# Casting DMAs from DRAM to DRAM in place of a packing pass through SBUF, in an attention and FFN block on one core

## What is computed

```
x = x + proj(quantise(concat(self_attention, cross_attention)))   # 8 groups, 2 heads each, 128 wide
x = x + down(silu(gate(layernorm(x))) * up(layernorm(x)))         # hidden size 1408
```

```
W = (wq.astype(float32) - ZERO_POINT) * scale[:, None]     # ZERO_POINT = 128
```

## Time and profile before

| what | value |
|---|---|
| median of 3 runs | 1793.88 us (1792.93 to 1796.43) |
| the profiled execution's own time | 1795.76 us |
| its span in the trace | 1793.9 us |
| TensorE's mean granted clock | 0.977 of full speed |
| busy share of the span: PE, DVE, ACT, POOL | 93%, 76%, 78%, 63% |
| DMA queue of SP | 254.71 MB, 71.0% of 16 engines |

### The profile page before, as it was taken

How to read it: one execution, slowest core, us unless ns; L and a number is a source line. 1 busy time by engine, 2 the same in 40 slices (tenths; PEclk the granted TensorE clock), 3 DMA queues, 4 the chain that set the end, 5 groups by cost and what they waited for, 6 DMA issues and landing times.

```text
span 1793.9 us, 44172 instructions
## 1 busy us (share of the span) xinstructions
PE 1675.9 (93%) x15776; PEld 1230.4 (69%) x15776; DVE 1364.5 (76%) x3181; ACT 1399.3 (78%) x2944; POOL 1138.4 (63%) x1043
## 2 busy tenths in 40 slices
PE   1449999999999999999999999999999979999999
PEld 1437778878887887788788877787888534444444
DVE  8969888997998799889979987997777652323232
ACT  6888999999999999999999999999999622121211
POOL 1137788778788877887787788778877613030202
PEclk9669999999999999999999999999999989999999
DMA  5557799888888988888798878888999970112100
GB/s 183 177 190 125 147 159 166 147 148 161 153 157 144 172 152 148 160 161 148 148 166 152 151 151 176 146 148 172 176 196 205 196 229 0 67 74 98 42 24 24
DMA packets 671666, 257.41 MB, mean 143 GB/s; under 512 B 616288, under 2 KB 634976, under 8 KB 671456
## 3 DMA queue, kind: packets, MB, share of 16 engines
q1 hardware_dynamic: 671456, 254.71, 71.0%
HBM read 74.10 MB, written 29.51 MB: 58 GB/s over the span
## 4 chain that ended last, share of the span: by engine, by line
ACT 28%; PE 21%; DVE 19%; POOL 15%; issue 10%; SPq 4%; DMA 3%; ACTq 0%; DVEq 0%; POOLq 0%
POOL local L1129 10%; ACT local L1041 7%; ACT local L1038 7%; ACT local L961 5%; PE ps_s L727 5%; DVE w_raw L1199 4%; ACT local L948 3%; DVE local L1371 2%; POOL w_raw L1113 2%; SPq L614 2%; DVE sq_sum L1284 2%; PE ps_pj L844 2%; PE ps_pj L845 2%; PE ps_o L844 2%; PE ps_o L845 2%
## 5 line engine op out<-in xcount | busy, mean ns | idle before, releaser
L1129 POOL TENSOR_TENSOR local<-local 128x512 bf16<-128x512 f32 x512 | 594.0, 1160 | 258.6 <-ACT local L1041 258.2
L720 PE MATMUL ps_pj<-wide 128*128 128x256 bf16 (+1 forms) x5544 | 584.9, 255 | 6.7 <-DVE wide L1208 4.0
L720 PEld LDWEIGHTS ps_pj<-wide 128*128 128x128 bf16 x5544 | 468.8, 98 | 116.8 <-ACT local L961 7.5
L1038 ACT ACTIVATE local<-ps_s,neg_max 128x512 f32<-128x512 f32 x512 | 380.5, 743 | 33.5 <-DVE neg_max L1363 30.4
L767 PE MATMUL ps_o<-v_hi,local 128*128 128x129 bf16 x2048 | 375.7, 221 | 7.6 <-DMA local<-local 5.6
L1041 ACT ACTIVATE local<-ps_s,neg_max 128x512 bf16<-128x512 f32 x512 | 382.5, 747 | 0.0
L769 PE MATMUL ps_o<-v_hi,local 128*128 128x129 bf16 x2048 | 375.3, 219 | 0.0
L768 PE MATMUL ps_o<-local 128*128 128x128 bf16 x2048 | 375.1, 218 | 0.0
L1363 DVE TENSOR_REDUCE neg_max<-ps_s 128x1 f32<-128x512 f32 x512 | 344.7, 673 | 37.2 <-PE ps_s L787 36.4
L961 ACT ACTIVATE local<-ps_pj,head_rstd 128x128 f32<-128x128 f32 x756 | 234.3, 416 | 51.6 <-issue 50.5
L1099 POOL TENSOR_TENSOR head_rstd<-sq_sum,minus_half 128x3 f32<-128x3 f32 x256 | 241.9, 945 | 27.3 <-DVE sq_sum L1284 27.3
(11 more groups left out here) (119 smaller groups left out, 2673.5 us busy)
## 6 DMA issues: line engine op xcount, KB each, us to landing
quantised_heads<-local SPq DMA_DIRECT2D x128, 128.0 KB, 2.5
w_raw<-w_group SPq DMA_DIRECT2D x56, 256.0 KB, 3.2
wide<-quantised_heads SPq DMA_DIRECT2D x3, 4096.0 KB, 13.1
local<-local SPq DMA_TRANSPOSE x640, 3.2
wide<-packed_weights SPq DMA_DIRECT2D x32, 256.0 KB, 3.2
wide<-x SPq DMA_DIRECT2D x7, 1024.0 KB, 8.6
w_raw<-w_proj SPq DMA_DIRECT2D x10, 512.0 KB, 4.5
wide<-quantised_heads SPq DMA_DIRECT2D x16, 256.0 KB, 3.4
```

What stands on the lines that cost most here:

```text
L720: last = mm(dst[:, at:at + n], lhs, w_at(par, part, c, cross * 512 + at, n), start=(k == 0), stop=(k == len(terms) - 1))
L1038: a(p_exp[:, u % 2], ps_s[u % 2][:], ACT.Exp, bias=neg_max[:, u % 4:u % 4 + 1])
L1129: tt_(pp[:, u % PP_BUFS, 1], p_exp[:, u % 2], pp[:, u % PP_BUFS, 0], ALU.subtract)\
```

## The change

GpSimd issues all conversions as DMAs whose source is float32 or int32 and whose destination is bf16, both in DRAM. `w_proj` goes in 8 DMAs of 4 rows per partition (512 KB written each, 1 MB read), ahead of the first `head_power`. The integers go in 22 DMAs, in slots 11, 35, 43 and 51 of groups 0 to 5, without the zero point; of these each waits for the one two before it. VectorE takes 128 off the loaded integers in place: 11 pieces of gate and up in the last group, each 6 slots after its load is issued, and 6 pieces of `w_down` after the last `z_rest` of batch 0. TensorE waits for VectorE's count in place of the landings. Both `pack` functions, `pre_load`, `pre_store`, `pack_load` and `pack_store` go, with the waits of the weight loads on them.

```diff
+            def cast_integers(n):
+                src, at = weight_piece(n)
+                if n >= 2:
+                    pool.wait_ge(int_out[n % 2], 16 * (n // 2))
+                dst = packed[:, at:at + src.shape[1] * src.shape[2]].rearrange("p (r w) -> p r w", w=src.shape[2])
+                nc.gpsimd.dma_start(dst, src).then_inc(int_out[n % 2], 16)
+
+            for n in range(CASTS):
+                rows = slice(CAST_ROWS * n, CAST_ROWS * (n + 1))
+                nc.gpsimd.dma_start(packed[:, 0:GU_AT].rearrange("p (f n) -> p f n", n=DM)[:, rows],
+                                    w_proj.rearrange("(f p) n -> p f n", p=P)[:, rows]).then_inc(cast_out[n], 16)
 
             for i in range(TILES):
                 head_power(i, i)
...
-                    for j, (_, pack_slot, _, _) in enumerate(PACK if not last else ()):
-                        if slot == pack_slot:
-                            pack(g, j)
+                    if slot in CAST_SLOTS and len(CAST_SLOTS) * g + CAST_SLOTS.index(slot) < PIECES:
+                        cast_integers(len(CAST_SLOTS) * g + CAST_SLOTS.index(slot))
...
-            def pack(i):
-                n = OPENING_PIECES[i]
-                act.wait_ge(pre_in[i % 3], 16 * (i // 3 + 1))
-                src, _, offset = weight_piece(n)
-                a(pre_buffer(i % 3)[:, 0:piece_size(n)].rearrange("p (r w) -> p r w", w=src.shape[2]),
-                  piece_raw(n, pre_buffer(i % 3)), ACT.Copy, bias=offset).then_inc(pre_done, 1)
...
-                for n in range(max(2 * i - 1, 0), 2 * i + 1):
-                    pack(n)
             head_norm(TILES - 1, TILES - 1, 0)
             ctx_part(2)
-            for n in range(2 * TILES - 1, len(OPENING_PIECES)):
-                pack(n)
...
-            pre_load(0)
-            load_ctx(1)
-            pre_load(1)
-            load_ctx(2)
-            pre_load(2)
-            for i in range(len(OPENING_PIECES)):
-                pre_store(i)
-                if 3 <= i + 2 < len(OPENING_PIECES):
-                    pre_load(i + 2)
-                if i == 4:
-                    load_ctx(3)
-            for i in range(len(OPENING_PIECES) - 3, len(OPENING_PIECES)):
-                sp.wait_ge(pre_out[i % 3], 16 * (i // 3 + 1))
-
+            for b in range(1, B):
+                load_ctx(b)
...
+            def take_offset(n):
+                for landed, count in tail_waits(n + 1):
+                    dve.wait_ge(landed, count)
+                view = tail_piece(n)[1]
+                v.tensor_scalar(view, view, -ZERO_POINT, None, ALU.add).then_inc(offset_done, 1)
...
+                    for n in range(WP_PIECES, X_FIRST):
+                        if last and slot == TAIL_SLOTS[n] + OFFSET_LAG:
+                            take_offset(n)
...
+            for n in range(X_DONE, X_DONE + WD_PIECES):
+                take_offset(n)
             dve.wait_ge(sdown_in, 16)
             hidden(0, 1)
```

More of the change, by code:

```diff
@@ L46 @@
 FP8_MAX = 448.0
+ZERO_POINT = 128.0
 EXPONENT = 0x7F80
@@ L57 @@
 QUANT_STEPS = 4
+CASTS = 8
 COLS = {}
@@ L285, in block_kernel @@
         heads_stored = sem("heads_stored")
[L286 to L291, removed]
+        cast_out = [sem(f"cast_out{i}") for i in range(CASTS)]
+        int_out = [sem(f"int_out{i}") for i in range(2)]
+        offset_done = sem("offset_done")
         tail_in = [sem(f"tail_in{i}") for i in range(2)]
@@ L325, in block_kernel @@
         WD_PIECES = -(-HC // 2)
[L326 to L331, removed]
+        PIECES = GU_PIECES + WD_PIECES
+        CAST_ROWS = G * HEADS // CASTS
+        CAST_SLOTS = (11, 35, 43, 51)
         SLOTS = B * UNITS
@@ L356, in block_kernel @@
         TAIL_SLOTS += [SLOTS + 6 + n for n in range(WD_PIECES)]
+        OFFSET_LAG = 6
         X_FIRST = WP_PIECES + CH * 2 * HID // GW
@@ L424, in tile_bank @@
             return START_BANKS[i % len(START_BANKS)] if at_start(t) else ps_pj[i % 2]
[L426 to L429, removed]
         def weight_piece(n):
-            if n < WP_PIECES:
-                return w_proj.rearrange("(f p) n -> p f n", p=P)[:, 2 * n:2 * n + 2], GW * n, 0.0
-            n -= WP_PIECES
             if n < GU_PIECES:
@@ L439, in weight_piece @@
                 src = (w_gate, w_up)[k].rearrange("(c p) n -> p c n", p=P)[:, c:c + 1, at:at + HID // 2]
-                return src, GU_AT + c * 2 * HID + k * HID + at, -128.0
+                return src, GU_AT + c * 2 * HID + k * HID + at
             n -= GU_PIECES
[L442 to L451, removed]
+            return w_down.rearrange("(c p) n -> p c n", p=P)[:, 2 * n:min(2 * n + 2, HC)], WD_AT + GW * n
         def tail_piece(n):
@@ L523, in _ @@
             load_weights(3)
-            def pre_load(i):
-                n = OPENING_PIECES[i]
[L527 to L537, removed]
-            pre_load(0)
-            load_ctx(1)
-            pre_load(1)
-            load_ctx(2)
-            pre_load(2)
-            for i in range(len(OPENING_PIECES)):
-                pre_store(i)
-                if 3 <= i + 2 < len(OPENING_PIECES):
-                    pre_load(i + 2)
-                if i == 4:
-                    load_ctx(3)
-            for i in range(len(OPENING_PIECES) - 3, len(OPENING_PIECES)):
-                sp.wait_ge(pre_out[i % 3], 16 * (i // 3 + 1))
+            for b in range(1, B):
+                load_ctx(b)
             def load_half(n, half):
@@ L557, in load_half @@
                 sp.wait_ge(w_ready, n - 1 + W_FREE)
[L558 to L562, removed]
                 at = slice(half * (GW // 2), (half + 1) * (GW // 2))
@@ L568, in _ @@
                     load_half(n, half)
[L570 to L584, removed]
             def tail_load(n):
@@ L588, in tail_load @@
                 if n == 0:
-                    sp.wait_ge(pack_out[0], 16 * 2 * (G - 1))
-                    sp.wait_ge(pack_out[1], 16 * (G - 1))
+                    for landed in cast_out:
+                        sp.wait_ge(landed, 16)
+                    for i, landed in enumerate(int_out):
+                        sp.wait_ge(landed, 16 * ((PIECES + 1 - i) // 2))
                 sp.wait_ge(proj_done, home_free(n))
@@ L619, in group @@
                             load_half(n, half)
[L620 to L624, removed]
                     if last and slot in TAIL_SLOTS:
@@ L863, in _ @@
                 turn_z(0, tt)
-            for landed, count in tail_waits(X_FIRST):
-                pe.wait_ge(landed, count)
+            pe.wait_ge(offset_done, X_FIRST - WP_PIECES)
             gate_up(0)
-            for landed, count in tail_waits(X_DONE + WD_PIECES):
-                pe.wait_ge(landed, count)
+            pe.wait_ge(offset_done, X_FIRST - WP_PIECES + WD_PIECES)
             with pe.Fori(1, B) as b:
```

## The result

The changed kernel takes 1818.79 us (median of 4, 1817.92 to 1821.0), the kernel before 1794.36 us: 24.4 us more, a ratio of 1.0134 with a 95% interval of 1.0121 to 1.0146. The forecast was 1824.6 us. The profiled execution took 1821.0 us, with a span of 1819.1.

A forecast was written before the change was run, and what follows sets the result against it. PE bounds the groups, so the opening decides: POOL held by casts until 121.9 us, plus 0.85 + 40, starts the groups 30.7 us later; other terms zero, 1793.9 + 30.7 = 1824.6 us, range 1796 to 1851.

The forecast's parts named there:

- The rule for the block: Opening: POOL issues each of the eight w_proj casts only after the one before landed, holding it until 121.9 us.
- The step from cast to cast: Opening, w_proj casts on POOL: 6.3 us landing plus 1.2 us issue, 7.5 us per cast.
- the lower bound of a serial step: Opening, w_proj casts: the shortest serial step is 6.3 us, issue inside, as a 1 MB context load lands.
- What is left after the block: Opening, after POOL leaves the casts: 0.85 us first `head_power` plus 40 us, mainly ACT's work, until the groups start.
- Its other signs: Trace: first `head_rstd` near 122 us, seven landings 7.5 us apart, first exponential near 163, then 1662 us to the end.
- Not held: Rival, opening: POOL issues eight casts back to back, groups start 13.4 us earlier, 1780.5 us; chance 0.15.
- Throughput: Rival, opening: descriptor space returns as rows are read, 3.6 us per cast, +3.4 us, 1797 us; chance 0.15.
- Slow casts: Rival, opening: DRAM-to-DRAM conversion takes 12.8 us a step, +68.6 us, 1862 us; chance 0.07 for above 11.3 us a step.
- The groups: Groups: packs removed and integer casts added on POOL beside a PE busy 99% of the stage, counted as zero.
- VectorE's subtractions: Last group, 4.7 us, and behind `z_rest`, 2.6 us, both covered by idle or waiting time, so zero.

The follow-up runs named there:

- The run with 2,048: Changed kernel with copies in place of transposing DMAs, `dynamic_dma_scratch_size` 2048 instead of 1024: 1792.39 us, 21.8 us below the same kernel at 1024.
- the casts alone: GpSimd alone issues 8 large, 16 half-size, 8 integer, then 8 large casts beside VectorE min/max; rest of the block left out: 47 us for the first eight.
- the control of before: Kernel before, with SP's 640 transposing DMAs replaced by plain copies of the same bytes: 1789.31 us, ratio 0.9955 to the kernel before.
- The two controls: Kernel before and changed kernel, each with SP's transposing DMAs replaced by plain copies: 1789.31 and 1814.19 us, medians 24.9 us apart.
- the moved casts: Changed kernel with copies for transposes, its eight w_proj casts moved ahead of GpSimd's second, third and fourth `power`: 1782.06 us without one 4946.64 us execution, ratio 0.9913.
- the control of the changed kernel: Changed kernel with SP's transposing DMAs replaced by plain copies: 1814.19 us, ratio 1.0098 to the kernel before.

## Why the prediction was right

**The rule for the block held.** The forecast's decisive choice, that each cast waits for the landing of the one before, is what the trace shows seven times. No row of the kernel before shows it: between no wait and a whole landing it was my estimate. The run with 2,048 shows what sets the wait, and the casts alone show that more of them find room when they are smaller. Counted in packets per DMA engine, 3 x 17 = 51 found room at 1,024 and 2 x 33 = 66 did not, and seven integer casts, 63, started before the first had landed; at 2,048, 3 x 33 = 99 found room and 4 x 33 = 132 did not. So my estimate from these runs is room for some 63 to 65 packets at 1,024, and for 99 to 131 at 2,048. No run shows what a cast puts into the room, or where it lies.

**The step from cast to cast was sized too high.** Forecast 7.5 us, measured 5.75 (5.0 of gap, 0.75 of issue). I had added a 1.2 us issue to 6.3 us taken from a 1 MB load into SBUF, and had called 6.3 with the issue inside the lower bound of a serial step. That bound was wrong as well. A cast landed in 5.5 us in the median, counted from the start of its issue of 0.75 us, and the next was issued 0.3 us later. One step was longer, 6.8 us: the second cast's issue took 1.75 us beside VectorE's quantising. GpSimd left at 110.3 us, not 121.9: 11.6 us less. That is the largest error of the sum.

**What is left after the block was sized too low.** Forecast 0.85 + 40 = 40.9 us, measured 154.64 - 110.27 = 44.4. ScalarE's work was nearly as forecast, 37.1 us for 36.5; its waits were 6.3 us for 3.4. The engine that I took as second, VectorE, has the main part in it: ScalarE waited 2.54 us for VectorE's `evacuate(4)`, which stands behind quantising in VectorE's queue. It waited 1.3 us more for later `head_power` steps, and 2.4 for TensorE as forecast. Summing one engine's work leaves such hand-overs out; I had allowed 1 us for them. The forecast had named this as a sign of being wrong: about 40 us should lie between the first `head_rstd` and the first exponential, and it was 44.4. Its other signs held: from the first exponential to the end it is 1664.5 us, 1661.8 before. The two errors, -11.6 and +3.5, make +22.5 of the forecast +30.7 us. That the total missed by only 6 us is in part luck: too long a hold was set off by too short a remainder and by a cost in the groups that I had put at zero.

**The rivals.** "Not held" needed less than 3.1 us from cast to cast. At 5.75 it did not come. The run with 2,048 comes near that rival's case by another way: 2.8 us a cast, first exponential 2.4 us ahead of the control of before. "Throughput" needed room to come back while rows are read; in the traces it came back with a whole landing, 0.3 us ahead of the next issue. Its price of 3.6 us a cast was too high too, as the 2.8 us show. "Slow casts", 12.8 us a step, is excluded: a cast landed in 5.5 us where the 1 MB loads of the context took 5.2 and 6.2 us in the same trace. A copy from DRAM to DRAM without conversion was not run.

**The groups were not free.** I counted zero for them, and they cost. Counting GpSimd's subtractions (L1129, in the changed kernel L1050) through both traces gives the lag of the changed kernel:

| subtraction | before, us | after, us | lag, us |
|---|---|---|---|
| first of group 0 | 133.5 | 156.0 | 22.5 |
| number 360, in group 5 | 1049.7 | 1081.3 | 31.6 |
| first of group 7 | 1280.4 | 1307.0 | 26.6 |

The two controls give 20.0, 26.9 and 21.8 us for the same three. Counted by the unit that is subtracted (0 to 63 in each group), the lag rises by 1.2 us at unit 15 of groups 0 to 4 and at unit 39 of groups 1 to 5, ten times in all, and by 0.2 to 0.3 us at the end of most groups. It falls at units 43, 51 and 59, where GpSimd's packs stood in the kernel before: by 0.3, 0.6 and 0.6 us with packs of 1.98 us, by 1.1, 1.4 and 1.4 with the packs of 2.78 us in group 6, whether or not a cast now stands in that slot; each time 0.2 us come back two units later. The pair of controls shows the same rises and falls from unit 3 on. At the first of the rises, unit 15 of group 0, only one VectorE line differs by more than 0.1 us (the kernel before, then the changed one):

```profile
168.35 1.88 DVE L1199 TENSOR_SCALAR w_raw<-w_raw,w_mean,wscale 128x128 f32<-128x128 f32 x4
```

```profile
191.53 2.95 DVE L1119 TENSOR_SCALAR w_raw<-w_raw,w_mean,wscale 128x128 f32<-128x128 f32 x4
```

The four scalings take 1.07 us more, about one GpSimd tensor instruction (1.16 us). VectorE does such a set of four in slots 7, 15, 27 and 39 of groups 0 to 6. At all ten rises the four take 2.94 to 2.97 us in place of 1.87 to 1.88, in both pairs of traces, and each time an integer cast was issued four slots before. Slots 7 and 27, which have no cast ahead, and group 6, which has no casts, keep their lengths. Two places with a cast ahead keep theirs too: slot 39 of group 0 and slot 15 of group 5. What makes the scalings longer is open: no row shows them waiting for GpSimd, and no kernel without the integer casts, or with them at other slots, was run, so their part in it is argued from the slots and not shown. What is measured is the result: my argument "PE is busy 99% of the stage, so nothing there counts" was wrong by 9 us up to group 5, of which 5 came back as the packs were gone.

**VectorE's subtractions cost nothing**, as forecast. The eleven in the last group were longer than thought, 10.4 us in all for the forecast 4.7, but the lag is 26.6 us at that group's start and 26.7 at the last `z_rest`. In front of the FFN the changed kernel was even 1.5 us quicker, because TensorE's clock came back sooner, 2.6 us after the first weight load of these projections and not 5.5: before, the projections of the first gate tile took 0.58 to 0.63 us each (nearly all of them 0.63), with a granted clock of 0.56 from 1470.7 to 1477.5 us, against 0.71 from 1497.4 to 1502.7 after; in the changed kernel TensorE, in order of time, went within them from 0.63 us, at a granted clock of 0.50 (1497.4 to 1500.1 us), to 0.38 us, at 1.00 (1500.9 to 1502.7 us):

```profile
1497.95 0.63 PE L774 MATMUL ps_pj<-local,wide 128*128 128x512 bf16 x1 [1.88 <-DVE wide L1276]
...
1500.09 0.56 PE L773 MATMUL ps_pj<-local,wide 128*128 128x512 bf16 x1
1500.48 0.38 PE L774 MATMUL ps_pj<-local,wide 128*128 128x512 bf16 x1
```

The first of these lines seems to say that TensorE waited for a subtraction. It did not: L773 and L774 take turns, the record of the L773 ahead is missing, and its weight load stands at 1497.54 us, 26.7 us after the one of before (1470.83), which is the lag of `z_rest`. Why the clock came back sooner is open.

## What to carry to other kernels

A DMA issued by GpSimd stands in GpSimd's queue, and GpSimd can be held ahead of it until an earlier DMA has landed, here for 5.0 us seven times: see in a trace how many go in a row before placing several, and give them either room or a place where GpSimd is idle. Here 2,048 in place of 1,024 in `dynamic_dma_scratch_size` was worth 21.8 us, and another place for the same eight instructions 32.1 us; the two together, and either with the transposes in the kernel, were not run, nor was a full block with sixteen half-size casts or with the casts of `w_proj` moved into the groups. Both cures leave the cost in the groups: with the moved casts the first exponential stands 12.4 us ahead of the control of before, and the time only 7.3. And a stage whose main engine is 99% busy was not free for the helpers here, 9 us up to group 5: follow one recurring instruction through both traces and read where the lag changes.

## What the runs showed of the hardware

- A cast from DRAM to DRAM that reads 1 MB and writes 512 KB landed 5.3 to 5.5 us after the start of its issue, in the median, with no other cast in flight, between the 5.2 and 6.2 us of two kinds of 1 MB context loads into SBUF, and cost 2.8 us in a filled queue. Beside SP's stores of 4 MB it took 9 us.
- A cast that found no room was issued 0.3 us after a landing: that of the cast one before with `dynamic_dma_scratch_size` at 1,024, that of the cast three before at 2,048, or at 1,024 with casts of half the size.
- Its issue kept GpSimd for 0.75 us, an integer cast of 128 rows for 0.6 us, where a pack of the same piece took 1.98 us.
- VectorE running 128x4096 bf16 min/max made the issue 1.6 us long in place of 0.75, 0.85 us more per cast. In the block it was one cast, and 1.0 us: the second, 1.75 us long beside VectorE's quantising on the same shape. In the control of the changed kernel that issue took 0.75 us, and it was VectorE's instruction that took 1.49 us in place of 1.22.
